# Inverse deviations spread over the partitions straight from SBUF, in place of a bounce through DRAM

## The chip, the cores and the metric

The kernel runs on one NeuronCore of a Trainium2 chip. The metric is the device time of one execution in microseconds (us). Before the change the median of three runs is 1423.2 us (1422.77 to 1428.34).

## What is computed

The input `x` is 32 images of 64 channels, 56 by 56 pixels, float32. A binarised 3x3 convolution with batch normalisation is added first; then each pixel, seen as a token of 64 channels, is normalised over its channels and goes through eight small expert networks. Cut to what matters here:

```python
x = x + conv_block(_ln_c(x), ...)                  # sign(x) * sign(w), batch norm, clip to [-1, 1]
t = _to_tokens(x)                                  # [32, 3136, 64]
u = (t - mean(t, -1)) / sqrt(var(t, -1) + 1e-5)    # _ln_t: over the 64 channels of one token
feat = mean(u, axis=0)                             # over the 32 images
w = softmax(feat @ Wr + br, axis=-1)               # one gate of 8 per pixel position
h = relu(bn1(u @ W1 + b1)); h = relu(bn2(h @ W2 + b2)); y = h @ Wo + bo    # 8 experts
x = _from_tokens(t + sum_over_experts(y * w))
```

The change lies in how `1/sqrt(var + 1e-5)`, one number per token, reaches the 64 partitions that hold the channels of that token.

## The kernel before, in words

SBUF has 128 partitions. Channels lie on partitions twice: partitions 0 to 63 hold the 64 channels of the even image rows, 64 to 127 those of the odd ones (`h` = 0 and 1). The first stage, up to about 204 us of the profile, is the convolution over 32 images; it leaves its output `y` in SBUF. The second stage is a sequence of 28 chunks (`body_of_chunks`, `RP` = 28), each with two image rows of all 32 images. All loops of this stage are unrolled. Each engine has a program of its own, and they meet in semaphores.

Within a chunk, 8 units (`u`) with 6 points each (48 half-points `h`) run the three expert layers: TensorE does `layer1`, `layer2` and `layer3` (L550, L572, L588), ScalarE evicts layer 1 (L743), VectorE evicts layer 2 and applies the gates (L936). Between these, `prep_point` puts the preparation of the next two chunks at half-points written out by hand in the table `STEADY`, which is counted over two chunks: an entry of 48 or more lies in the chunk just ahead of the one that is prepared, at that number less 48. For chunk `q` = `k` + 1, prepared during chunk `k`:

- `var` = 52: four matmuls (L614) sum the squares over the channels; ScalarE makes logarithm, copy, exponential and square of the result (L770 to L777), the inverse deviations `rs`;
- `inv` = 60 and 62: VectorE corrects them by one Newton step (L963 to L968) and signals `rs_done`. `rs` then holds eight useful rows of 448 floats (1792 bytes): partition 32*i + h is the row for image group i (0 to 3) and half h;
- `spread_rs` (L296 to L305), on SyncE (SP) whose queue issues the DMAs, copies each of these rows to 64 partitions of the tile `spread`. Groups 0 and 1 are step `p` = 0, groups 2 and 3 are `p` = 1;
- `norm` (L432 to L435) on GpSimd (POOL) multiplies the centred tokens `xc` of step `p` by `spread` as soon as `rb_loaded[p]` says that it is there, and signals `u_done[p]`;
- `feature` (L439 to L449), next on POOL, sums the normalised tokens over the images (four additions), which needs both steps, and signals `feat_done`;
- `logits` = 87: TensorE waits for `feat_done` and multiplies by the gate weights (L626); softmax, `turn` (L633) and `wb` (L639) follow at 90 to 95, before the next chunk's first units need the gates.

The order on POOL in a chunk is written out too: three `add_const`, the last group's `add_upper` of the chunk before, `add_const`, `add_upper(k, 0)`, then the two `norm` and `feature` of chunk k + 1, then `add_upper(k, 1)` and `add_upper(k, 2)` (L465), after each of which SP stores a quarter of the chunk. SP's order is: load of the first half of chunk k + 2 (L287), store of the chunk before (L312), load of the second half, `spread_rs` of chunk k + 1, three stores. The tile `spread` has a second use: ScalarE writes the squares of chunk k + 2 into it (L762, at half-points 33 and 45 of chunk k) after waiting for `u_done[p]` of chunk k + 1.

The normalisation of chunk 0 has no chunk to hide in: it runs between the end of the convolution and the first unit (`prep_ahead`), and so do `spread_rs(0, 0)` and its two `norm`.

Of the kernel before, what the change touches and what calls it, by code (L numbers as in the profile page):

```python
# [5 lines left out]
F32 = mybir.dt.float32  # L6
# [9 lines left out]
B, C, H, W = 32, 64, 56, 56  # L16
# [8 lines left out]
STEPS = 2  # L25
G = 4
BG = B // G
NG = BG * W
# [22 lines left out]
def metaformer_kernel(nc, x, cw, gamma, beta, Wr, br, W1, b1, g1, be1, m1, v1, W2, b2, g2, be2, m2, v2, Wo, bo, out):  # L51
    with ExitStack() as ctx:
        def sb(name, shape, dt, to=ctx):
            return to.enter_context(nc.sbuf_tensor(name, shape, dt))

        def sem(name):
            return ctx.enter_context(nc.semaphore(name))
# [37 lines left out]
        h = sb("h", [P, 2, 2, 2, NG], F32)  # L95
# [16 lines left out]
        o = sb("o", [P, B, W], F32)  # L112
        t = sb("t", [P, G, NG], F32)
        xc = sb("xc", [P, 2, STEPS, 2, NG], F32)
        spread = sb("spread", [P, STEPS, 2, NG], F32)
        rs = sb("rs", [P, NG], F32)
# [9 lines left out]
        wb = sb("wb", [P, 2, PAIRS, 2, W], F32)  # L126
        gconst = sb("gconst", [P, 2, W], F32)

        rs_rows = nc.dram_tensor("rs_rows", [2, 2, STEPS, 2, NG], F32).ap()

        ps = ctx.enter_context(nc.psum_tensor("ps", [P, 8, 512], F32))
        L1_BANKS, L2_BANKS, ACC_BANKS = 0, (2, 4), 6
# [34 lines left out]
        root_done = sem("root_done")  # L167
        rs_done = sem("rs_done")
        d_rs = sem("d_rs")
        rs_kept = sem("rs_kept")  # L170
        rb_loaded = [sem(f"rb_loaded{p}") for p in range(STEPS)]
        u_done = [sem(f"u_done{p}") for p in range(STEPS)]
        feat_done = sem("feat_done")
# [54 lines left out]
        def body_of_chunks(chunk):  # L228

            for k in range(RP):  # L230
                chunk(k, k % 2, k == 0, min(RP - 1 - k, 2))
# [26 lines left out]
        with nc.Block() as block:  # L258


            @block.sync
            def _(sp):
                for s in stored:
                    sp.sem_inc(s, 16)
                for h in range(2):
                    sp.dma_start(cwt[64 * h:64 * h + 64], cw).then_inc(s_cw, 16)
                    sp.dma_start(gb[64 * h:64 * h + 64, 0:1], gamma.rearrange("(c o) -> c o", o=1)).then_inc(s_cw, 16)

                def load_image(b, slot):

                    xb = x_pairs[b] if isinstance(b, int) else x_pairs[bass.ds(b, 1)].rearrange("o c k t w -> (o c) k t w")
                    sp.dma_start(xa[0:64, slot, 1:SLOTS, :], xb[:, :, 1, :]).then_inc(s_xa[slot], 16)
                    sp.dma_start(xa[64:128, slot, 0:RP, :], xb[:, :, 0, :]).then_inc(s_xa[slot], 16)

                sp.wait_ge(s_zero, 1)
                for b in range(XRING):
                    load_image(b, b)
                with sp.Fori(0, B // XRING - 1) as r:
                    for i in range(XRING):
                        sp.wait_ge(a_split, XRING * r + i + 1)  # L280
                        load_image(XRING * r + XRING + i, i)

                def load_half(q, s, p):
                    images = slice(2 * BG * p, 2 * BG * p + 2 * BG)
                    xq = x[images, :, bass.ds(2 * q, 2), :] if not isinstance(q, int) else x[images, :, 2 * q:2 * q + 2, :]
                    for h in range(2):
                        sp.dma_start(xin[64 * h:64 * h + 64, s, images], xq[:, :, h, :].rearrange("b c w -> c b w")).then_inc(x_loaded[p], 16)  # L287

                sp.wait_ge(a_split, B - XRING + XIN_OVER)
                for q in range(2):  # L290
                    for p in range(STEPS):
                        if q:
                            sp.wait_ge(x_loaded[p], 32)
                        load_half(q, q, p)

                def spread_rs(q, s):  # L296

                    sp.wait_ge(rs_done, q + 1)
                    for i in range(2 * STEPS):
                        sp.dma_start(rs_rows[s, :, i // 2, i % 2], rs[32 * i:32 * i + 2, :]).then_inc(rs_kept, 16)  # L300
                    sp.wait_ge(rs_kept, 32 * STEPS * q + 32 * STEPS)
                    for p in range(STEPS):
                        for h in range(2):
                            sp.dma_start(spread[64 * h:64 * h + 64, p],
                                         rs_rows[s, h, p:p + 1].broadcast_to([C, 2, NG])).then_inc(rb_loaded[p], 16)  # L305

                def store(k, g):
                    images = slice(BG * g, BG * g + BG)
                    oq = out[images, :, bass.ds(2 * k, 2), :] if not isinstance(k, int) else out[images, :, 2 * k:2 * k + 2, :]
                    sp.wait_ge(sum_done, G * k + g + 1)  # L310
                    for h in range(2):
                        sp.dma_start(oq[:, :, h, :].rearrange("b c w -> c b w"),  # L312
                                     o[64 * h:64 * h + 64, images]).then_inc(stored[g], 16)

                def chunk(k, s, first, left):
                    if left > 1:
                        sp.wait_ge(x1g_done, G * k + 2)
                        load_half(k + 2, s, 0)
                    if not first:
                        store(k - 1, G - 1)  # L320
                    if left > 1:
                        sp.wait_ge(x1g_done, G * k + G)
                        load_half(k + 2, s, 1)
                    if left:
                        spread_rs(k + 1, 1 - s)
                    for g in range(G - 1):
                        store(k, g)
                    if not left:
                        store(k, G - 1)

                spread_rs(0, 0)
                body_of_chunks(chunk)
                for s in stored:
                    sp.wait_ge(s, 32 * RP + 16)
# [3 lines left out]
            def _(pool):  # L338
# [92 lines left out]

                def norm(q, s, p):  # L432

                    pool.wait_ge(rb_loaded[p], 32 * q + 32)
                    nc.gpsimd.tensor_tensor(xc[:, s, p], xc[:, s, p], spread[:, p], ALU.mult).then_inc(u_done[p], 1)  # L435

                FEAT_STEPS = 3
# [29 lines left out]
                def chunk(k, s, first, left):  # L467
                    for g in range(G - 1):
                        add_const(k, s, g)
                    if not first:  # L470
                        add_upper(k - 1, G - 1)
                    add_const(k, s, G - 1)
                    add_upper(k, 0)
                    if left:
                        for p in range(STEPS):
                            norm(k + 1, 1 - s, p)
                        feature(k + 1, 1 - s)
                    add_upper(k, 1)
                    add_upper(k, 2)
                    if not left:  # L480
                        add_upper(k, G - 1)

                for p in range(STEPS):
                    norm(0, 0, p)
# [552 lines left out]
```

## Time and profile before

| | |
|---|---|
| median of 3 runs | 1423.2 us |
| the profiled execution's own time | 1421.64 us |
| its span, first to last instruction | 1419.7 us |
| TensorE busy | 1344.9 us (95%) |
| VectorE, ScalarE, GpSimd busy | 971.1, 885.3, 553.2 us |
| moved by DMA | 107.08 MB, mean 75 GB/s |
| mean granted TensorE clock | 0.984 |

All times below are of the one profiled execution, counted from the start of its span. A row of a timeline gives the start, the duration, the engine, the source line, the operation, the output tile and its inputs, and in brackets the idle time of the engine before it with what ended that. Issue instructions on SP show when a DMA is handed over, not when its data lands.

### The profile page before, as it was taken

Reading aid. Unit: us, or ns where it says so; the run is one execution under the profiler, and the core shown is the slowest. Engines: PE = TensorE matmul, PEld = TensorE weight load, DVE = VectorE, ACT = ScalarE, POOL = GpSimd, SP = SyncE. Lnnn points to the kernel's source line nnn. Section 1 sums busy time; section 2 is a strip of 40 time slices with the busy share of each in tenths; the row PEclk is TensorE's granted clock in tenths of the full one; section 3 lists DMA queues with packets and bytes.
Section 4 is the critical chain, followed back from the end, with each engine's and each line's share of the span. In section 5 each row is a group of like instructions: output and inputs, shape, how many; then the busy total and the mean of one; then the engine's idle time right before and its main releaser. Section 6 shows DMA issues by size and latency. Waiting matters only on the chain. (4 is left out here: it accounts for less than half of the span.)

```text
span 1419.7 us, 34136 instructions
## 1 busy us (share of the span) xinstructions
PE 1344.9 (95%) x12984; PEld 667.3 (47%) x12984; DVE 971.1 (68%) x1660; ACT 885.3 (62%) x1279; POOL 553.2 (39%) x474
## 2 busy tenths in 40 slices
PE   3999973999999999999999999999999999999998
PEld 2666651544444544445444444444544454444444
DVE  5888872676767666666666666676766767666665
ACT  3666664666666666656666666666666666666653
POOL 7000052434444443444343344444434444434441
PEclk9999995999999999999999999999999999999999
DMA  9999931232233333223333233233333323332221
GB/s 159 176 151 149 143 52 27 60 79 61 55 71 67 73 73 80 52 61 73 67 72 75 61 65 68 62 78 69 77 66 61 66 60 73 73 80 48 53 49 32
DMA packets 361597, 107.08 MB, mean 75 GB/s; under 512 B 353552, under 2 KB 353776, under 8 KB 361456
## 3 DMA queue, kind: packets, MB, share of 16 engines
q1 hardware_dynamic: 360192, 103.49, 38.9%
q0 software_dynamic: 1264, 1.61, 0.7%
q8 instruction: 101, 1.65, 0.5%
q14 instruction: 40, 0.33, 0.1%
HBM read 78.97 MB, written 26.09 MB: 74 GB/s over the span
## 5 line engine op out<-in xcount | busy, mean ns | idle before, releaser
L936 DVE SCALAR_TENSOR_TENSOR v<-ps,negb,wb 128x448 f32<-128x448 f32 x896 | 571.0, 678 | 300.9 <-PE ps L572 300.1
L743 ACT ACTIVATE h<-ps,bias 128x896 f32<-128x896 f32 x448 | 451.3, 1007 | 318.9 <-PE ps L550 318.9
L550 PE MATMUL ps<-xc,w 64*64 64x448 f32 x3584 | 458.1, 541 | 13.1 <-POOL xc L435 11.3
L588 PE MATMUL ps<-v,wo 64*64 64x448 f32 x3584 | 454.7, 540 | 3.4 <-issue 2.9
L572 PE MATMUL ps<-h,w 64*64 64x448 f32 x3584 | 450.9, 540 | 4.9 <-issue 2.5
L588 PEld LDWEIGHTS ps<-v,wo 64*64 64x64 f32 x3584 | 169.9, 133 | 187.5 <-issue 174.6
L550 PEld LDWEIGHTS ps<-xc,w 64*64 64x64 f32 x3584 | 162.3, 132 | 185.2 <-issue 179.4
L572 PEld LDWEIGHTS ps<-h,w 64*64 64x64 f32 x3584 | 166.0, 133 | 160.3 <-issue 146.7
L465 POOL TENSOR_TENSOR o<-o,upper 128x448 f32<-128x448 f32 x112 | 127.4, 1137 | 284.3 <-DVE o L946 284.3
L457 POOL TENSOR_TENSOR o<-xin,gconst 128x448 f32<-128x448 f32 x112 | 130.2, 1182 | 236.0 <-ACT gconst L786 143.3
L435 POOL TENSOR_TENSOR xc<-xc,spread 128x896 f32<-128x896 f32 x56 | 121.5, 2187 | 172.0 <-DMA spread<-rs_rows 172.0
L518 PE MATMUL ps<-sgn,convw 128*128 128x392 bf16 x768 | 135.1, 332 | 0.0
L712 ACT ACTIVATE y<-ps 128x392 f32 (+1 forms) x128 | 63.3, 498 | 59.8 <-PE ps L518 59.8
L518 PEld LDWEIGHTS ps<-sgn,convw 128*128 128x128 bf16 x768 | 72.6, 98 | 55.7 <-issue 6.2
L749 ACT ACTIVATE upper<-ps 128x448 f32<-128x448 f32 x112 | 60.5, 541 | 55.5 <-PE ps L588 55.5
L957 DVE SCALAR_TENSOR_TENSOR xin<-t,xin 128x448 f32<-128x448 f32 x112 | 88.5, 793 | 1.0 <-ACT t L767 0.9
L875 DVE BATCH_NORM_STATS2 stats<-y (+1 forms) x128 | 69.0, 562 | 22.5 <-ACT y L712 22.1
L767 ACT ACTIVATE t<-y,bn 128x448 f32<-128x448 f16 x112 | 83.3, 749 | 0.1
L946 DVE TENSOR_TENSOR o<-ps,o 128x448 f32<-128x448 f32 x112 | 68.9, 615 | 18.6 <-PE ps L588 18.6
L606 PE MATMUL ps<-xin,centre 64*64 64x448 f32 x448 | 62.5, 560 | 7.2 <-DVE xin L957 4.3
L758 ACT ACTIVATE xc<-ps 128x896 f32<-128x896 f32 x56 | 51.4, 918 | 28.4 <-PE ps L606 28.4
L704 ACT ACTIVATE sgn<-ps 128x392 bf16<-128x392 f32 (+1 forms) x128 | 55.5, 526 | 13.9 <-PE ps L509 13.7
(151 smaller groups left out, 837.8 us busy)
## 6 DMA issues: line engine op xcount, KB each, us to landing
xa<-in_x SPq DMA_DIRECT2D x64, 392.0 KB, 6.3
xin<-in_x SPq DMA_DIRECT2D x112, 224.0 KB, 4.1
spread<-rs_rows SPq DMA_DIRECT2D x112, 224.0 KB, 4.1
out<-o SPq DMA_DIRECT2D x224, 112.0 KB, 2.5
rs_rows<-rs SPq DMA_DIRECT2D x112, 3.5 KB
rows<-in_L_ffn_g POOLq DMA_DIRECT2D x2, 256.0 KB, 6.1
rows<-in_L_ffn_v POOLq DMA_DIRECT2D x2, 256.0 KB, 7.2
cwt<-in_L_conv_weight SPq DMA_DIRECT2D x2, 144.0 KB, 2.6
```

What stands on the lines that cost most here:

```text
L435: nc.gpsimd.tensor_tensor(xc[:, s, p], xc[:, s, p], spread[:, p], ALU.mult).then_inc(u_done[p], 1)
L457: nc.gpsimd.tensor_tensor(o[:, images, :], xin[:, s, images, :], gconst[:, s:s + 1, :].broadcast_to([P, BG, W]), ALU.add).then_inc(x1g_don ...
L465: nc.gpsimd.tensor_tensor(og, og, upper[:], ALU.add).then_inc(sum_done, 1)
L518: last = mm(at, convw[:, kx, nxt, :], sgn[:, i % 2, KG * g + nxt:KG * g + nxt + KG, kx:kx + W], start=(kx + nxt == 0), stop=(kx + nxt == 3))
L550: last = mm(ps[64 * two:64 * two + 64, L1_BANKS + ab, 0:NG], w1[half, P * q + C * two:P * q + C * two + C], xc[half, s, g // 2, ab ^ (g % ...
L572: last = mm(ps[64 * i:64 * i + 64, L2_BANKS[ab] + low, 0:NG], w2[rows_, Q + QUADS * i, :], h[rows_, u % 2, i, ab, :], start=True, stop=True)
L588: last = mm(ps[64 * par:64 * par + 64, ACC_BANKS + low, 0:NG], wo[rows_, 2 * Q + d, :], v[rows_, u % 2, par ^ (g % 2), d, :], start=(Q == ...
L743: A(h[:, u % 2, i], ps[:, L1_BANKS:L1_BANKS + 2, 0:NG], ACT.Relu, bias=bias[:, 0, q:q + 1]).then_inc(h_done[i], 1)
L767: A(t[:, g].rearrange("p (b w) -> p b w", w=W), yq, ACT.Relu, bias=OFFSET1, scale=SCALE).then_inc(t_done, 1)
L875: last = V.bn_stats(sb_, yb)
L936: last = V.scalar_tensor_tensor(out=v[:, u % 2, ab, d, :].rearrange("p (b w) -> p b w", w=W), in0=ps[:, L2_BANKS[ab] + d, 0:NG].rearrange( ...
L957: V.scalar_tensor_tensor(out=xg, in0=t[:, g].rearrange("p (b w) -> p b w", w=W), scalar=2.0, in1=xg, op0=ALU.min, op1=ALU.add).then_inc(x1 ...
```

## The change

The DRAM tensor `rs_rows`, its semaphore and the four small DMAs that wrote it are gone, and with them SP's wait for them. Each of the four 224 KB loads, which read two rows of DRAM for 64 partitions, becomes two DMAs of 112 KB; each of these reads one row of `rs`, 1792 bytes on one SBUF partition, 64 times over, and writes it to 64 partitions of `spread`. `rb_loaded[p]` now counts four DMAs.

```diff
-        rs_rows = nc.dram_tensor("rs_rows", [2, 2, STEPS, 2, NG], F32).ap()
...
                     sp.wait_ge(rs_done, q + 1)
                     for i in range(2 * STEPS):
-                        sp.dma_start(rs_rows[s, :, i // 2, i % 2], rs[32 * i:32 * i + 2, :]).then_inc(rs_kept, 16)
-                    sp.wait_ge(rs_kept, 32 * STEPS * q + 32 * STEPS)
-                    for p in range(STEPS):
                         for h in range(2):
-                            sp.dma_start(spread[64 * h:64 * h + 64, p],
-                                         rs_rows[s, h, p:p + 1].broadcast_to([C, 2, NG])).then_inc(rb_loaded[p], 16)
+                            sp.dma_start(spread[64 * h:64 * h + 64, i // 2, i % 2],
+                                         rs[32 * i + h:32 * i + h + 1, :].rearrange("o (a n) -> o a n", a=1).broadcast_to([1, C, NG])).then_inc(rb_loaded[i // 2], 16)
...
-                    pool.wait_ge(rb_loaded[p], 32 * q + 32)
+                    pool.wait_ge(rb_loaded[p], 64 * q + 64)
```

The order on SP, in the program before, around the first two calls of `spread_rs` (the tile `xin` takes the input for the residual):

```order
L287 DMA xin<-in_x 64x16x56
L300 DMA rs_rows<-rs 2x448 [waits rs_done]
L300 DMA rs_rows<-rs 2x448 x3
L304 DMA spread<-rs_rows 64x896 [waits rs_kept]
L304 DMA spread<-rs_rows 64x896 x3
L287 DMA xin<-in_x 64x16x56 [waits x1g_done]
```

The same place in the changed program, up to the stores of the first chunk (its lines are numbered two to five lower):

```order
L285 DMA xin<-in_x 64x16x56
L299 DMA spread<-rs 64x1x448 [waits rs_done]
L299 DMA spread<-rs 64x1x448 x7
L285 DMA xin<-in_x 64x16x56 [waits x1g_done]
L285 DMA xin<-in_x 64x16x56
L285 DMA xin<-in_x 64x16x56 [waits x1g_done]
L285 DMA xin<-in_x 64x16x56
L299 DMA spread<-rs 64x1x448 [waits rs_done]
L299 DMA spread<-rs 64x1x448 x7
L307 DMA out<-o 64x8x56 [waits sum_done]
```

Eight DMAs with one wait stand where there were eight with two; what comes before and after them on SP is the same, and no other engine's order moves.

## Rows read from the trace of the kernel before

**Rows 1.** The page: the span, and the engines' busy time in it

```profile
span 1419.7 us, 34136 instructions
PE 1344.9 (95%) x12984; PEld 667.3 (47%) x12984; DVE 971.1 (68%) x1660; ACT 885.3 (62%) x1279; POOL 553.2 (39%) x474
```

**Rows 2.** Windows by stage: us, busy of each engine, PEclk, DMA share, GB/s

```profile
840.91:881.57 40.66, 40.53 (x430) 17.92 (x433) 27.98 (x52) 27.09 (x36) 17.91 (x14) 1.00 0.33 70
256.29:1340.23 1083.94, 1070.04 (x11072) 503.29 (x11074) 742.01 (x1326) 703.21 (x936) 467.28 (x362) 1.00 0.32 68
```

**Rows 3.** Waits of all engines: us in total, times, longest us

```profile
POOL xc L435 <- DMA spread<-rs_rows: 172.0, 30, 25.7
...
PE ps L550 <- POOL xc L435: 11.3, 1, 11.3
...
PE ps L626 <- POOL feat L449: 4.6, 5, 2.0
```

**Rows 4.** Waits of SP's queue: us in total, times, longest us

```profile
SPq L304 <- DMA rs_rows<-rs: 64.4, 28, 2.7
```

**Rows 5.** Timeline of a middle chunk: SP, POOL, ScalarE and TensorE

```profile
766.20 1.13 SPq L300 DMA_DIRECT2D rs_rows<-rs  x4
769.68 2.40 SPq L304 DMA_DIRECT2D spread<-rs_rows  x4
...
774.46 4.46 POOL L435 TENSOR_TENSOR xc<-xc,spread 128x896 f32<-128x896 f32 x2 [5.18 <-DMA spread<-rs_rows]
779.05 2.08 POOL L444 TENSOR_TENSOR feat<-xc 128x896 f32<-128x896 f32 x1
...
783.44 0.42 POOL L449 TENSOR_TENSOR feat<-feat 128x112 f32<-128x112 f32 x1
783.82 1.14 POOL L465 TENSOR_TENSOR o<-o,upper 128x448 f32<-128x448 f32 x1
...
782.06 0.94 ACT L762 ACTIVATE spread<-xc 128x896 f32<-128x896 f32 x1
...
785.51 0.34 PE L626 MATMUL ps<-wr,feat 64*56 64x8 f32 x7
```

**Rows 6.** Timeline of two other chunks: end of the feature, start of the logits

```profile
867.42 0.42 POOL L449 TENSOR_TENSOR feat<-feat 128x112 f32<-128x112 f32 x1
868.07 0.34 PE L626 MATMUL ps<-wr,feat 64*56 64x8 f32 x7
...
1199.65 0.42 POOL L449 TENSOR_TENSOR feat<-feat 128x112 f32<-128x112 f32 x1
1202.16 0.34 PE L626 MATMUL ps<-wr,feat 64*56 64x8 f32 x7
```

**Rows 7.** Timeline ahead of the first chunk

```profile
227.48 1.19 SPq L300 DMA_DIRECT2D rs_rows<-rs  x4
...
229.62 2.40 SPq L304 DMA_DIRECT2D spread<-rs_rows  x4
...
234.41 4.10 POOL L435 TENSOR_TENSOR xc<-xc,spread 128x896 f32<-128x896 f32 x2 [25.66 <-DMA spread<-rs_rows]
236.62 1.77 PE L550 MATMUL ps<-xc,w 64*64 64x448 f32 x8 [11.34 <-POOL xc L435]
...
242.74 0.42 POOL L449 TENSOR_TENSOR feat<-feat 128x112 f32<-128x112 f32 x1
...
244.49 0.38 PE L626 MATMUL ps<-wr,feat 64*56 64x8 f32 x8
...
260.56 0.96 PE L588 MATMUL ps<-v,wo 64*64 64x448 f32 x8
```

**Rows 8.** DMA issues: KB each, median us from issue to landing

```profile
spread<-rs_rows SPq DMA_DIRECT2D x112, 224.0 KB, 4.1
out<-o SPq DMA_DIRECT2D x224, 112.0 KB, 2.5
rs_rows<-rs SPq DMA_DIRECT2D x112, 3.5 KB
```

**Rows 9.** Windows in bursts of the spread: DMA share and GB/s last

```profile
230.50:233.50 3.00, 0.00 (x0) 0.00 (x0) 0.00 (x0) 0.00 (x0) 0.00 (x0) 0.50 0.86 209
270.40:270.90 0.50, 0.50 (x10) 0.45 (x8) 0.50 (x2) 0.41 (x1) 0.00 (x0) 1.00 0.52 208
```

**Rows 10.** Windows ahead of the first chunk: TensorE idle, then busy again

```profile
226.00:228.00 2.00, 0.00 (x0) 0.00 (x0) 1.93 (x5) 2.00 (x4) 0.00 (x0) 1.00 0.00 0
230.00:232.00 2.00, 0.00 (x0) 0.00 (x0) 0.00 (x0) 0.00 (x0) 0.00 (x0) 0.50 0.51 129
250.00:252.00 2.00, 2.00 (x14) 0.72 (x15) 0.00 (x0) 0.65 (x2) 0.50 (x1) 0.50 0.00 0
252.00:254.00 2.00, 1.71 (x16) 0.66 (x12) 0.55 (x1) 1.01 (x1) 2.00 (x3) 0.86 0.00 0
```

More of the change, by code:

```diff
@@ L169, in metaformer_kernel @@
         d_rs = sem("d_rs")
-        rs_kept = sem("rs_kept")
         rb_loaded = [sem(f"rb_loaded{p}") for p in range(STEPS)]
```

## The prediction
> **What bounds the kernel now.** I read the page first: TensorE is busy for 1344.9 of 1419.7 us [rows 1]. The windows by stage say how closely: over 26 chunks it works 1070.04 of 1083.94 us at the full clock, so a chunk lasts 41.7 us, and in the best one it works 40.53 of 40.66 us [rows 2]. In these chunks nothing but TensorE's own work can be shortened by more than half a microsecond each. The list of waits then shows who could hold it up. POOL waits 172.0 us for the spread rows, the longest wait on a DMA [rows 3], but POOL is not the bound, so that costs nothing by itself. What it leads to costs: TensorE waits 4.6 us in 5 places for the sum over the images, and 11.3 us once, ahead of the first chunk, for the first normalised tokens [rows 3].
>
> The timeline of a middle chunk gives the path and its slack. SP hands over the small DMAs at 766.20, waits for them, hands over the four loads from 769.68; POOL starts `norm` at 774.46, ends the feature at 783.86, and TensorE takes it at 785.51 [rows 5]. From SP's first issue to the end of the feature that is 17.7 us. The slack behind it is 1.65 us here; over the 28 chunks it runs from 0.2 (868.07 less 867.84) to 2.1 us (1202.16 less 1200.07) [rows 6], and I take 0.9 us for all. So this path is off the critical one by less than a microsecond: saving on it buys almost nothing, and a delay beyond 0.9 us is paid in full, once per chunk.
>
> **What goes.** The four small DMAs and the wait for them: 3.48 us from 766.20 to 769.68 [rows 5], with 64.4 us of waiting over the 28 calls [rows 4]. Nothing that TensorE does depends on them except through this path.
>
> **What comes.** Eight DMAs of 112 KB where four of 224 KB stood. Four loads are handed over in 2.40 us [rows 5], 0.6 each, so eight take 4.8 us; that ends at 4.8 us after the first issue, where before it ended at 5.9. The issue is no price. The stores queued behind them on SP can be handed over a microsecond earlier.
>
> The price is the transfer. The bytes that are written stay the same: 8 x 64 x 1792 = 917,504. What is new is where they are read: each of the eight DMAs reads one row on a single SBUF partition, 64 times, for all DMA engines at once. No row of this trace shows many engines on one partition. The bounds, from the nearest rows: at best it goes as from DRAM, where a load lands 4.1 us after its issue [rows 8] and the burst runs at 209 GB/s [rows 9]. At worst one partition serves its readers one after the other, at what one DMA engine draws: in the best half-microsecond of a burst a busy engine moves 208 / (0.52 x 16) = 25 GB/s, over three microseconds 209 / (0.86 x 16) = 15 GB/s [rows 9]. The small DMAs, two partitions each, are the only reads of `rs` in the trace, 3.5 KB each [rows 8], too short to say which holds; the stores [rows 8] draw on 64 partitions at once.
>
> I take the one-engine rate, the better value of 25 GB/s, because the sixteen engines reach 209 GB/s in the loads of before with all of DRAM behind them and 64 partitions in front, while here the whole burst has one narrow source at a time. 917,504 bytes at 25 GB/s are 36.7 us. A rule of the Trainium skill speaks against the change in the same way ("SBUF — State Buffer", section "Door 1: The DMA port swizzle"): partitions share 16 DMA ports of about 27.2 GB/s each, and by its formula rows 0, 1, 32 and 33 lie on one port and 64, 65, 96 and 97 on another. By that figure the transfer would be an estimated 33.7 us and the sum below 84 us less; if the two ports worked side by side it would be 17 us. No row here tells these apart.
>
> **The sum.** Data starts to flow about 1 us after the first issue (in 230 to 232 us the engines are busy for half of the window, the first load having been handed over at 229.62) [rows 7, 10]. The last row lands 37.7 us after the first issue; `norm` of the second step takes 2.1 us (half of the 4.10 of both) [rows 7]; from the end of `norm`, 778.92, to the end of the feature, 783.86, it is 4.9 us [rows 5]. Together 44.7 us, against 17.7 plus 0.9 of slack: TensorE waits 26.1 us at the logits of each of 27 chunks, 705 us. Some of this wait moves forward, since ScalarE may not write the next squares into `spread` (782.06) [rows 5] before `norm` is done; it is the same wait, not a second one. `add_upper` of the next group stands behind the feature on POOL (783.82) [rows 5]; its 1.1 us and its store come later by the same 26 us, and the stop of TensorE covers them.
>
> Ahead of the first chunk, SP starts at 227.48 and the feature ended at 243.16; now it ends at 272.2, less 1.3 us of slack before 244.49 [rows 7]: 28 us. The first `norm` no longer decides there, since the feature needs both steps.
>
> TensorE's clock: it stops at full clock (1.00 in 226 to 228), is granted half (0.50, 1.2 of 2.4 GHz) while still idle in 230 to 232, and after a stretch of steady work from 250 us is at 0.86 in 252 to 254 [rows 10]. Eight matmuls take 1.77 us at half and 0.96 us at full clock [rows 7]. I charge 1.5 us for each of 28 stops, 42 us; the bounds are 0 and 4 us (0 to 112).
>
> 1421.6 (the profiled execution) + 705 + 28 + 42 = 2197 us; I say **2195 us**. The median of the runs shown, 1423.2, is 1.6 us above the profiled one.
>
> **The rivals.**
>
> *Unhindered.* The direct read goes as fast as the read from DRAM. Then the path shortens by about 2 us: p = 0 lands about 2.5 us after its fourth issue at 2.4 us [rows 5, 8], 5 us in place of the 6.9 between 227.48 and 234.41 [rows 7]. The head gains 2 us, the 5 waits of 4.6 us [rows 3] go, and the time is 1415 us. It speaks for it that the bytes, the engines and the written partitions are the same; against it, the single source. It decides at 0.9 us of slack: the transfer may last 17.7 + 0.9 - 2.1 - 4.9 - 1 = 10.6 us, 87 GB/s, before TensorE feels it; above that rate the change is never slower. The Trainium skill has a rule on that side as well ("DMA: Bandwidth & Descriptors", section "Where 436 GB/s comes from"): between SBUF and SBUF the fabric's 435 GB/s binds, an estimated 2.1 us for these bytes. Chance 0.17.
>
> *In part hindered.* A partition gives more than one engine's worth, or the two pairs of rows flow side by side, two to three and a half times 25 GB/s. At 50 GB/s the transfer is 18.4 us, the feature ends after 26.4 us, 7.8 too late: 28 x 7.8 = 218, 1640 us, up to 1680 with the clock. At 75 GB/s it is 12.2 us, 1.6 too late, 1467 us. Chance 0.05.
>
> *Worse than one engine's best.* Readers disturb each other and the burst runs at 20 GB/s: 45.9 us, 9.2 more for each of 28, 2450 us. It belongs to the forecast's own range.
>
> **How the numbers follow.** One source at a time: 0.78, its own range 1800 to 2450 us, with about 0.02 above it. In part: 0.05, of which the part above 1600 is in the range. Unhindered: 0.17, left out whole. The range is 1600 to 2450 us. About 0.5% (7 us) is what a measurement of this kernel can tell from no change. The unhindered case, 1415 us, is 0.45 to 0.6% below, so it is split: 0.07 faster, 0.10 the same; all else, 0.83, is slower.
>
> **What would show it.** In the profile after: landing of the spread's DMAs far above 4.1 us, growing from the first to the eighth, with a DMA share near 1 and only about 25 GB/s for some 37 us in each chunk; POOL's wait for `spread` near 28 x 30 us; TensorE waiting for the feature (or for ScalarE behind `norm`) some 25 us in every chunk, chunks of about 68 us; the granted clock at half after each stop. The forecast is wrong if the landing stays below some 10 us, in which case TensorE's 41 us per chunk stand and only the head moves; its size is wrong if the burst's GB/s is far from 25.

## The result and the profile after

The changed kernel takes 2085.14 us (median of 4 runs, 2084.86 to 2086.99) against 1423.45 us before: a ratio of 1.4625 (95% interval 1.4593 to 1.4658). It is 662 us slower; 2195 was forecast, 1600 to 2450 the range.

The page of the changed kernel answers to [rows 1]:

```profile
span 2082.9 us, 34136 instructions
PE 1476.5 (71%) x12984; PEld 739.5 (36%) x12984; DVE 962.5 (46%) x1660; ACT 885.8 (43%) x1279; POOL 539.1 (26%) x474
```

The windows by stage, to be read beside the second row of [rows 2] (us, busy time of each engine, granted clock, DMA share, GB/s): the first is the same 26 chunks, from the first to the last ScalarE read of the variances; the second is four microseconds within one burst of the spread, when the input's load had landed and no store had been handed over.

```profile
282.47:1977.94 1695.47, 1193.35 (x11072) 573.33 (x11074) 733.02 (x1326) 703.64 (x935) 454.89 (x362) 0.84 0.54 43
1016.00:1020.00 4.00, 2.12 (x12) 0.98 (x15) 0.44 (x1) 0.00 (x0) 0.00 (x0) 0.69 0.87 27
```

A chunk now lasts 1695.47 / 26 = 65.2 us, 23.5 more than before. The DMA engines are busy for 87% of that window and move 27 GB/s, where they moved 209 GB/s at 86% [rows 9]: they wait for data. The list of waits, to be read beside [rows 3]:

```profile
POOL xc L430 <- DMA spread<-rs: 814.4, 56, 37.2
...
PE ps L621 <- POOL feat L444: 353.9, 27, 16.6
PE ps L583 <- issue: 65.7, 14, 7.9
...
PE ps L545 <- issue: 53.1, 13, 6.8
...
ACT spread L757 <- POOL xc L430: 37.0, 9, 6.6
PE ps L567 <- issue: 34.9, 9, 8.4
...
PE ps L545 <- POOL xc L430: 22.9, 1, 22.9
```

TensorE's wait for the feature has grown from 4.6 to 353.9 us, in 27 places: 13.1 us each. The timeline of a middle chunk of the changed kernel, in the order of [rows 5]:

```profile
1009.54 23.18 SPq L299 DMA_DIRECT2D spread<-rs  x8
1032.77 24.50 SPq L307 DMA_DIRECT2D out<-o  x6
...
1028.00 2.08 POOL L430 TENSOR_TENSOR xc<-xc,spread 128x896 f32<-128x896 f32 x1 [15.38 <-DMA spread<-rs]
1043.54 2.07 POOL L430 TENSOR_TENSOR xc<-xc,spread 128x896 f32<-128x896 f32 x1 [13.45 <-DMA spread<-rs]
...
1049.82 0.42 POOL L444 TENSOR_TENSOR feat<-feat 128x112 f32<-128x112 f32 x1
...
1050.39 0.42 PE L621 MATMUL ps<-wr,feat 64*56 64x8 f32 x5 [9.72 <-POOL feat L444]
```

The two `norm` start 18.5 and 34.0 us after SP's first issue, and the feature ends after 40.7 us, where it took 17.7. In the DMA issues, against [rows 8], the landing has gone from 4.1 to 14.4 us for half the bytes per DMA:

```profile
spread<-rs SPq DMA_DIRECT2D x224, 112.0 KB, 14.4
out<-o SPq DMA_DIRECT2D x224, 112.0 KB, 2.5
```

The stores read 64 partitions per DMA and land as before. So reading SBUF by DMA is not slow as such. What is slow about these reads was open: the number of DMAs (theory C below), the way from SBUF to SBUF (D), the single partition (A2), or the DMA port on which that partition lies (A1).

### The profile page after: what moved, and what is told of

It is laid out like the page before. It is cut to its first block and busy times, and to the rows that moved or that the text cites. A ratio compares the mean times of both kernels' runs of the same rounds, so it can differ in the third digit from the quotient of the medians.

```text
span 2082.9 us, 34136 instructions
## 1 busy us (share of the span) xinstructions
PE 1476.5 (71%) x12984; PEld 739.5 (36%) x12984; DVE 962.5 (46%) x1660; ACT 885.8 (43%) x1279; POOL 539.1 (26%) x474
## 5 line engine op out<-in xcount | busy, mean ns | idle before, releaser
L545 PE MATMUL ps<-xc,w 64*64 64x448 f32 x3584 | 519.7, 580 | 76.0 <-issue 53.1
L583 PE MATMUL ps<-v,wo 64*64 64x448 f32 x3584 | 523.6, 588 | 66.2 <-issue 65.7
L567 PE MATMUL ps<-h,w 64*64 64x448 f32 x3584 | 520.3, 590 | 37.3 <-issue 34.9
L430 POOL TENSOR_TENSOR xc<-xc,spread 128x896 f32<-128x896 f32 x56 | 116.2, 2075 | 814.4 <-DMA spread<-rs 814.4
L583 PEld LDWEIGHTS ps<-v,wo 64*64 64x64 f32 x3584 | 197.9, 144 | 273.5 <-issue 253.9
L545 PEld LDWEIGHTS ps<-xc,w 64*64 64x64 f32 x3584 | 189.6, 144 | 268.2 <-issue 256.9
L621 PE MATMUL ps<-wr,feat 64*56 64x8 f32 x224 | 15.7, 238 | 364.5 <-POOL feat L444 353.9
L567 PEld LDWEIGHTS ps<-h,w 64*64 64x64 f32 x3584 | 187.7, 145 | 207.4 <-issue 191.4
L621 PEld LDWEIGHTS ps<-wr,feat 64*56 64x56 f32 x224 | 13.9, 198 | 389.4 <-issue 389.2
L941 DVE TENSOR_TENSOR o<-ps,o 128x448 f32<-128x448 f32 x112 | 69.4, 620 | 40.1 <-PE ps L583 39.8
L601 PE MATMUL ps<-xin,centre 64*64 64x448 f32 x448 | 72.8, 607 | 19.7 <-issue 14.3
## 6 DMA issues: line engine op xcount, KB each, us to landing
spread<-rs SPq DMA_DIRECT2D x224, 112.0 KB, 14.4
```

Of the source, the lines that this page charges most:

```text
L545: last = mm(ps[64 * two:64 * two + 64, L1_BANKS + ab, 0:NG], w1[half, P * q + C * two:P * q + C * two + C], xc[half, s, g // 2, ab ^ (g % ...
L567: last = mm(ps[64 * i:64 * i + 64, L2_BANKS[ab] + low, 0:NG], w2[rows_, Q + QUADS * i, :], h[rows_, u % 2, i, ab, :], start=True, stop=True)
L583: last = mm(ps[64 * par:64 * par + 64, ACC_BANKS + low, 0:NG], wo[rows_, 2 * Q + d, :], v[rows_, u % 2, par ^ (g % 2), d, :], start=(Q == ...
L601: last = mm(ps[64 * high:64 * high + 64, Z + low, 0:NG], centre64[rows_, :], xin[rows_, s, BG * g:BG * g + BG, :], start=True, stop=True)
L941: V.tensor_tensor(og, ps[:, ACC_BANKS, 0:NG], og, ALU.add).then_inc(out_done, 1)
```

## The experiments

The kernel before was timed beside each experiment on the same chip; ratios are against that.

### The split alone

The kernel before, its loads from DRAM halved (`rb_loaded[p]` counts four DMAs here too):

```diff
                         for h in range(2):
-                            sp.dma_start(spread[64 * h:64 * h + 64, p],
-                                         rs_rows[s, h, p:p + 1].broadcast_to([C, 2, NG])).then_inc(rb_loaded[p], 16)
+                            for a in range(2):
+                                sp.dma_start(spread[64 * h:64 * h + 64, p, a],
+                                             rs_rows[s, h, p, a:a + 1].broadcast_to([C, NG])).then_inc(rb_loaded[p], 16)
...
```

> The kernel before with its four loads from DRAM split into eight of 112 KB, as the change has them; the bounce through DRAM stays. Theory A (the single SBUF source is what costs): the time stays at 1423 us, within 5 us, since the eight hand-overs take some 5 us of SP in place of 2.4 and the path has under 1 us of slack in some chunks; landing near 4 us. Theory C (eight DMAs of 112 KB are what costs, by number or by form): near the changed kernel, above 1700 us.

1427.99 us, ratio 1.0011 (0.9997 to 1.0025). Eight DMAs in this form cost nothing that can be told. TensorE waits for the feature 11.2 us in 12 places in place of 4.6 in 5, which shows how little slack there is. Theory C falls.

### Sixteen source partitions per DMA

Each row of `rs` exists 16 times, since the variance matmul (same shape, 565 ns in place of 566) now fills all its 32 columns:

```diff
-                    nc.gpsimd.memset(var_ones[64 * h:64 * h + 64, h:h + 3:2], 1.0 / C).then_inc(s_const, 1)
+                    nc.gpsimd.memset(var_ones[64 * h:64 * h + 64, h:32:2], 1.0 / C).then_inc(s_const, 1)
...
-                                         rs[32 * i + h:32 * i + h + 1, :].rearrange("o (a n) -> o a n", a=1).broadcast_to([1, C, NG])).then_inc(rb_loaded[i // 2], 16)
+                                         rs[32 * i + h:32 * i + 32:2, :].rearrange("o (a n) -> o a n", a=1).broadcast_to([16, C // 16, NG])).then_inc(rb_loaded[i // 2], 16)
```

> The changed kernel with each row of rs made 16 times over (the weights of the variance matmul filled in all 32 columns, alternating by half, at no cost on TensorE), and each of the eight DMAs reads 16 partitions, two apart, four times each, in place of one partition 64 times. Theory A (one port or one partition is the source that saturates): the burst runs above 150 GB/s, POOL's first norm starts about 5 to 6 us after SP's first issue, and the time is 1412 to 1423 us. Theory D (a copy from SBUF to SBUF is slow in itself): it stays above 1800 us.

1424.79 us, ratio 0.9995 (0.9981 to 1.0008). A window inside a burst, and the DMA issues, of this run:

```profile
600.60:604.60 4.00, 4.00 (x48) 1.84 (x44) 3.06 (x6) 3.14 (x4) 1.79 (x2) 1.00 0.97 221
...
spread<-rs SPq DMA_DIRECT2D x224, 112.0 KB, 2.8
```

221 GB/s in all, of which the spread's own packets are 200 (the rest is the end of the input's load), from SBUF to SBUF, to the same destinations: theory D falls, and the whole 662 us are the narrow source. But the 1412 to 1423 us that a fast read was to give did not come; that question is taken up below.

### Four sources, adjacent or apart

On top of the filled columns, the source alone differs:

```diff
-rs[32 * i + h:32 * i + 32:2, :].rearrange("o (a n) -> o a n", a=1).broadcast_to([16, C // 16, NG])
+rs[32 * i:32 * i + 4, :].rearrange("o (a n) -> o a n", a=1).broadcast_to([4, C // 4, NG])
```

for the adjacent ones (half of the copies then carry the rows of the other half `h`, which changes what is computed but no order or size), and for those apart

```diff
-rs[32 * i + h:32 * i + 32:2, :].rearrange("o (a n) -> o a n", a=1).broadcast_to([16, C // 16, NG])
+rs[32 * i + h:32 * i + 32:8, :].rearrange("o (a n) -> o a n", a=1).broadcast_to([4, C // 4, NG])
```

> As the kernel with 16 sources, but each DMA reads the four adjacent partitions 32*i to 32*i+3, each 16 times; only every second of these rows belongs to the half it is written to, so the normalisation of the tokens gets deviations of the other half in part. Theory A1 (the limit belongs to the DMA port, which adjacent partitions share): burst near 29 GB/s, 2050 to 2110 us. Theory A2 (the limit belongs to the single partition or its address): four times the rate, near 100 GB/s or what four DMA engines draw, 9 us of transfer, 1415 to 1450 us.

> As the kernel with four sources, but the four partitions are eight apart (32*i + h and 8, 16 and 24 above it), which by the map of the SBUF page lie on four ports. Theories A1 and A2 agree: near 100 GB/s, 9 us of transfer, the feature ends 17 us after SP's first issue as before, 1415 to 1450 us. If four sources mean only that four DMA engines take part and these are slow by themselves, it is far above that, and the run with four adjacent sources says nothing on the port.

Adjacent: 2213.87 us, ratio 1.5526 (1.5476 to 1.5575), above the expected 2050 to 2110. Eight partitions apart: 1453.0 us, ratio 1.0190 (1.0157 to 1.0223), just above the expected 1450. The waits of the second, and a window inside one of its bursts:

```profile
POOL xc L430 <- DMA spread<-rs: 228.1, 56, 25.4
...
PE ps L621 <- POOL feat L444: 29.6, 26, 2.4
...
656.00:660.00 4.00, 4.00 (x42) 2.35 (x39) 2.75 (x6) 1.38 (x3) 1.29 (x1) 1.00 0.26 98
```

Both use four partitions, each read 16 times, in the same number of DMAs. Only the distance between the partitions differs, and it makes 761 us. Theory A2, a limit of the single partition, falls: four adjacent ones together are no faster than one. The limit is shared by neighbours, as a port is; that it is the port and not something else with the same grouping, no run can tell. The adjacent run is in fact slower than one partition read 64 times; both `norm` of a chunk show by how much:

```profile
642.03 24.03 SPq L299 DMA_DIRECT2D spread<-rs  x8
...
662.19 2.07 POOL L430 TENSOR_TENSOR xc<-xc,spread 128x896 f32<-128x896 f32 x1 [17.07 <-DMA spread<-rs]
...
679.82 2.07 POOL L430 TENSOR_TENSOR xc<-xc,spread 128x896 f32<-128x896 f32 x1 [15.57 <-DMA spread<-rs]
```

The second starts 37.8 us after the first issue; less about 1 us of start, 917,504 bytes in 36.8 us are 25 GB/s, against 28 in the changed kernel (33.0 us in the chunk above). Windows inside this burst, the first with other traffic in it, the second without, show a DMA share of a quarter, as much as four engines of sixteen, where the changed kernel has 0.87:

```profile
645.00:675.00 30.00, 16.26 (x163) 9.34 (x152) 10.86 (x18) 10.15 (x12) 2.19 (x2) 0.80 0.25 31
650.00:656.00 6.00, 6.00 (x69) 4.47 (x65) 4.25 (x8) 3.71 (x5) 0.00 (x0) 1.00 0.23 25
```

The run with the partitions apart has the same share, 0.26, and moves 98 GB/s with it. So the number of DMA engines at work does not explain the adjacent run. In these traces a packet of the spread (one row, 1792 bytes) takes 74 ns with the partitions apart, 260 ns with four adjacent ones and 928 ns in the changed kernel (medians inside a burst): the more engines draw on one place, the longer each of them waits for the same row.

### Half of it direct

Step 0 by the direct read, step 1 through DRAM:

```diff
-                    for i in range(2 * STEPS):
+                    for i in range(2, 4):
                         sp.dma_start(rs_rows[s, :, i // 2, i % 2], rs[32 * i:32 * i + 2, :]).then_inc(rs_kept, 16)
+                    for i in range(2):
+                        for h in range(2):
+                            sp.dma_start(spread[64 * h:64 * h + 64, 0, i],
+                                         rs[32 * i + h:32 * i + h + 1, :].rearrange("o (a n) -> o a n", a=1).broadcast_to([1, C, NG])).then_inc(rb_loaded[0], 16)
-                    sp.wait_ge(rs_kept, 32 * STEPS * q + 32 * STEPS)
-                    for p in range(STEPS):
+                    sp.wait_ge(rs_kept, 32 * q + 32)
+                    for p in (1,):
...
-                    pool.wait_ge(rb_loaded[p], 32 * q + 32)
+                    pool.wait_ge(rb_loaded[p], (64, 32)[p] * (q + 1))
```

> Step 0 direct from one SBUF partition per DMA as in the changed kernel, step 1 by the bounce through DRAM as before: half of the narrow reads. If the price is bytes over the rate of one port, the narrow part lasts 15.5 us (half of the 31 of the changed kernel), the rest 2 to 3 us behind it in the same rings; the feature ends 1 + 15.5 + 2.5 + 2.1 + 4.9 = 26 us after SP's first issue, 7.4 us too late, 28 times: 1630 us, up to 1670 with the clock. If the price were a fixed one per chunk, not one per byte, it would be near 2085 us.

1727.97 us, ratio 1.2146 (1.2034 to 1.2258): above the 1630 to 1670 that were expected. A chunk of it:

```profile
645.89 0.81 SPq L300 DMA_DIRECT2D rs_rows<-rs  x2
646.75 7.18 SPq L303 DMA_DIRECT2D spread<-rs  x4
653.98 8.38 SPq L308 DMA_DIRECT2D spread<-rs_rows  x2
...
665.42 4.54 POOL L439 TENSOR_TENSOR xc<-xc,spread 128x896 f32<-128x896 f32 x2 [16.44 <-DMA spread<-rs]
...
674.20 0.42 POOL L453 TENSOR_TENSOR feat<-feat 128x112 f32<-128x112 f32 x1
```

The feature ends 28.7 us after SP's first issue, not 26: the small DMAs go first, `norm` of step 0 starts after 19.5 us. That is 10.1 us beyond the 18.6 that are free, 283 us in 28 places; 1424 and 283 make 1707, and the other 21 us fit a clock charge of under a microsecond per stop. Half of the narrow bytes cost 303 of 662 us, so the price goes with the bytes and not with the chunk. The two loads from DRAM took SP 4.2 us each to hand over where the kernel before needs 0.6.

### Eight ports, one per DMA

One partition per DMA again, with the filled columns, but at 0, 5, 40, 45, 80, 85, 120 and 125, so that by the port map named below each of the eight lies on a port of its own ("four apart" in the expectation is the step of the added offset, not the distance):

```diff
-rs[32 * i + h:32 * i + h + 1, :]
+rs[32 * i + h + 4 * (2 * i + h):32 * i + h + 4 * (2 * i + h) + 1, :]
```

> As the changed kernel, one partition per DMA read 64 times, but the eight source partitions are four apart, each on a port of its own by the map of the SBUF page. If the DMA engines work through the DMAs one after the other (rings in order), the one port in use at a time still sets the rate: burst of 28 to 31 us, 1990 to 2085 us. If the DMAs flow side by side, the burst is shorter than 10 us and the time 1420 to 1480 us.

### The order of the groups

```diff
-                    for i in range(2 * STEPS):
+                    for i in (0, 2, 1, 3):
```

> The changed kernel with its eight DMAs in the order groups 0, 2, 1, 3: DMAs of the one port (groups 0 and 1) alternate with those of the other (2 and 3), two by two. If rings in order set the pace: both steps end near 30 us, so the feature ends as in the changed kernel, 2060 to 2100 us, a little more since the first norm starts later and ScalarE waits for it longer. If the two ports work side by side: burst near 16 us, 1600 to 1680 us.

The first took 1645.77 us (ratio 1.1568, 1.1412 to 1.1724), the second 1909.35 us (1.3421, 1.3311 to 1.3530). Neither is where one of the two theories put it. A chunk of the kernel with a port per DMA:

```profile
620.17 12.48 SPq L299 DMA_DIRECT2D spread<-rs  x8
631.86 2.08 POOL L430 TENSOR_TENSOR xc<-xc,spread 128x896 f32<-128x896 f32 x1 [8.61 <-DMA spread<-rs]
638.04 2.28 POOL L430 TENSOR_TENSOR xc<-xc,spread 128x896 f32<-128x896 f32 x1 [4.10 <-DMA spread<-rs]
```

and of the interleaved one:

```profile
636.86 19.60 SPq L299 DMA_DIRECT2D spread<-rs  x8
...
657.56 2.09 POOL L430 TENSOR_TENSOR xc<-xc,spread 128x896 f32<-128x896 f32 x1 [17.61 <-DMA spread<-rs]
...
663.94 2.07 POOL L430 TENSOR_TENSOR xc<-xc,spread 128x896 f32<-128x896 f32 x1 [4.29 <-DMA spread<-rs]
```

Less 1 us of start, the transfers last 16.9 and 26.1 us, where the changed kernel's last 33.0. By the port map of the Trainium skill ("SBUF — State Buffer", section "Door 1: The DMA port swizzle") the source moves to another port once in the changed kernel, 3 times in the interleaved one and 7 times here. Per further passage that is (33.0 - 26.1) / 2 = 3.5 and (26.1 - 16.9) / 4 = 2.3 us saved (3.1 and 2.3 by the means of 27 chunks, 32.4, 26.2 and 17.0). So a DMA and the one behind it in the queue do overlap, as long as they draw on different ports, but far from all eight at once. This says again that it is the port: the changed kernel's groups 0 and 1 read partitions 0, 1, 32 and 33, four different ones, and gain nothing from the overlap: on average the first three DMAs of the changed kernel land 4.2 us apart, 27 GB/s, and only towards the one passage the steps get shorter (3.4 and 3.7 us). If 32 and 33 were elsewhere than 0 and 1, the changed kernel would have had the interleaved one's three passages, and its time.

### Why the fast direct read gains nothing, and a version that does

With 16 sources the path is shorter than in the kernel before, and the time is the same. The groups of that kernel that changed:

```profile
L952 DVE SCALAR_TENSOR_TENSOR xin<-t,xin 128x448 f32<-128x448 f32 x112 | 125.4, 1123 | 1.0 <-ACT t L762 0.9
L601 PE MATMUL ps<-xin,centre 64*64 64x448 f32 x448 | 62.4, 576 | 11.7 <-issue 6.0 <-DVE xin L952 4.3 <-ACT xc L753 1.1
```

VectorE's addition on the residual (`x1`) takes 1123 ns; in the kernel before the same groups read:

```profile
L957 DVE SCALAR_TENSOR_TENSOR xin<-t,xin 128x448 f32<-128x448 f32 x112 | 88.5, 793 | 1.0 <-ACT t L767 0.9
L606 PE MATMUL ps<-xin,centre 64*64 64x448 f32 x448 | 62.5, 560 | 7.2 <-DVE xin L957 4.3 <-issue 1.6 <-ACT xc L758 1.1
```

Now that POOL starts `norm` earlier, its work falls onto more of the `x1`; in the changed kernel, where POOL mostly waits, they take 678 ns. The Trainium skill has a rule for such a meeting ("SBUF — State Buffer", section "Who interferes with whom"): a two-input operation of VectorE and one of GpSimd that reads SBUF exclude each other on a shared pair of ports. The durations agree: an `x1` that meets no instruction of POOL takes at most 626 ns in every kernel here (70 of them in the kernel before, 34 with 16 sources), and one that meets POOL up to 2.5 us (42 of mean 1090 ns, and 78 of mean 1343). That the two exclude each other, and do not merely slow each other down, no run measured.

What this does to TensorE shows in one distance. After the third `x1` of a chunk VectorE has two evictions `v` to do, and with 16 sources TensorE's first centring matmul (L601) starts 1.29 us after the end of that `x1` in 23 of 27 chunks; in the kernel before it does so in 3. The profile puts this idle time down to "issue", ten times and 4.3 us in all, in place of once. From the logits of the second chunk to those of the last, the windows of the kernel before and of the one with 16 sources read:

```profile
283.48:1366.80 1083.32, 1069.81 (x11072) 500.33 (x11069) 740.50 (x1322) 699.51 (x930) 469.62 (x365) 1.00 0.32 67
282.39:1368.51 1086.12, 1074.39 (x11075) 496.80 (x11069) 770.75 (x1322) 699.89 (x930) 475.98 (x364) 1.00 0.33 67
```

Its idle time has fallen from 13.5 to 11.7 us (the waits for the feature went from 4.6 to 0.3 us, the ones behind `x1` came), but it is busy for 4.6 us more with the same matmuls at the same clock. The held matmuls may be part of that, but no row says so.

I went on from a wider form of the direct read, one DMA of 224 KB per group:

```diff
-                    nc.gpsimd.memset(var_ones[64 * h:64 * h + 64, h:h + 3:2], 1.0 / C).then_inc(s_const, 1)
+                    nc.gpsimd.memset(var_ones[64 * h:64 * h + 64, 16 * h:16 * h + 16], 1.0 / C).then_inc(s_const, 1)
...
-                        for h in range(2):
-                            sp.dma_start(spread[64 * h:64 * h + 64, i // 2, i % 2],
-                                         rs[32 * i + h:32 * i + h + 1, :].rearrange("o (a n) -> o a n", a=1).broadcast_to([1, C, NG])).then_inc(rb_loaded[i // 2], 16)
+                        sp.dma_start(spread[:, i // 2, i % 2],
+                                     rs[32 * i:32 * i + 32, :].rearrange("o (a n) -> o a n", a=1).broadcast_to([32, 4, NG])).then_inc(rb_loaded[i // 2], 16)
...
-                    pool.wait_ge(rb_loaded[p], 64 * q + 64)
+                    pool.wait_ge(rb_loaded[p], 32 * q + 32)
```

> The weights of the variance matmul filled so that 16 of each 32 rows of rs belong to the one half and 16 to the other; one DMA per group reads 32 partitions four times each and writes all 128 partitions of spread: four DMAs of 224 KB, no bounce. Hand-over 2.4 us in place of 4.8. Transfer as fast as in the kernel with 16 sources; if what held that one back is that its norm meets VectorE's additions on the residual (its L952 took 1123 ns against 793 in the kernel before), this one is no better: 1421 to 1427 us. If the hand-over mattered: 1415 to 1420 us.

1425.61 us, ratio 1.0005 (0.9994 to 1.0016): no gain. Then three tries with the table, on top of it, the first being

```diff
-            t=(12, 15, 18, 21), x1=(20, 24, 26, 32), centre=(31, 43), power=(33, 45),
+            t=(4, 7, 18, 21), x1=(9, 12, 30, 34), centre=(31, 43), power=(33, 45),
```

> The kernel with four wide DMAs, and VectorE's additions on the residual (x1) moved out of the stretch in which POOL now runs norm and feature: half-points 9, 12, 30, 34 in place of 20, 24, 26, 32, and ScalarE's t at 4, 7, 18, 21. If the collision of VectorE and POOL took the gain away, x1 takes under 750 ns, TensorE no longer waits for it at L601, and the time is 1408 to 1418 us, better than the kernel before. If TensorE's own work sets a chunk, it stays at 1420 to 1427 us. If ScalarE or VectorE is now late at the units where t and x1 were put, it is slower than 1430 us.

1432.54 us, ratio 1.0063 (1.0048 to 1.0079). The meeting did become rarer (910 ns in place of 1071), yet the time rose. The second, `x1=(20, 24, 30, 34)` and `t` as it was:

> The kernel with four wide DMAs, with only the second pair of VectorE's residual additions moved: half-points 20, 24, 30, 34 in place of 20, 24, 26, 32, so that the third no longer falls into POOL's feature. If the meeting with POOL costs, x1's mean falls from 1071 ns and the time is 1 to 5 us below the kernel with four wide DMAs. If TensorE's own work and its eviction set a chunk, no change, 1421 to 1428 us.

1419.3 us beside 1427.41 us of the kernel before: ratio 0.9948 (0.9929 to 0.9966), the one kernel of the study that is faster. The third, `t=(8, 11, 18, 21)`, `x1=(13, 16, 30, 34)`:

> As before, with both pairs outside POOL's norm and feature (x1 at 13, 16, 30, 34) and t at 8, 11, 18, 21, closer to the old places than in the slower try with 9 and 4. If it was the early places (4 to 9, beside the load of the input and POOL's additions) that cost 7 us there, this one is at 1415 to 1423 us; if any place away from the tuned ones costs, near 1432 us.

1438.62 us, ratio 1.0083 (1.0064 to 1.0102). What each does to TensorE is in the groups of `x1` and of the centring matmuls behind it. With four wide DMAs and the old table:

```profile
L951 DVE SCALAR_TENSOR_TENSOR xin<-t,xin 128x448 f32<-128x448 f32 x112 | 119.6, 1071 | 1.0 <-ACT t L761 0.9
L600 PE MATMUL ps<-xin,centre 64*64 64x448 f32 x448 | 62.3, 573 | 10.3 <-issue 4.9 <-DVE xin L951 4.3 <-ACT xc L752 1.1
```

with the late pair:

```profile
L951 DVE SCALAR_TENSOR_TENSOR xin<-t,xin 128x448 f32<-128x448 f32 x112 | 117.7, 1054 | 1.0 <-ACT t L761 0.9
L600 PE MATMUL ps<-xin,centre 64*64 64x448 f32 x448 | 62.9, 568 | 6.8 <-DVE xin L951 4.3 <-issue 1.4 <-ACT xc L752 1.1
```

and with both pairs moved (the `x1` group, and a row of the list of waits):

```profile
L951 DVE SCALAR_TENSOR_TENSOR xin<-t,xin 128x448 f32<-128x448 f32 x112 | 84.6, 758 | 1.0 <-ACT t L761 0.9
...
PE ps L582 <- DVE v L930: 21.4, 26, 1.2
```

The last of these is the clearest: `x1` is quicker than in the kernel before (758 ns against 793), but its first pair, put at half-points 13 and 16, stands beside the Newton step (half-points 12 and 14) and delays VectorE's eviction `v` ahead of layer 3, and TensorE waits for that in 26 places. So the length of `x1` was the wrong measure; where it stands in VectorE's queue counts. In the kernel with the late pair it is no shorter (1054 ns against 1071) and its third one still meets POOL, but it is no longer ahead of the first centring matmul: that starts 1.29 us behind it in 12 of 27 chunks with the old table, in none with the new one. The idle time before L600 falls from 10.3 to 6.8 us, back to about the 7.2 of the kernel before. What puts the late pair ahead of the kernel before is then the shorter path itself. The same stretch as above reads

```profile
282.74:1361.45 1078.71, 1069.38 (x11074) 510.44 (x11069) 763.18 (x1322) 699.95 (x930) 479.12 (x364) 1.00 0.32 67
```

TensorE is busy as long as in the kernel before and idle for 9.3 us in place of 13.5: the waits for the feature are gone. That and 0.7 us ahead of it are the 5.0 us between the two profiled executions (spans of 1414.7 and 1419.7 us). The last run is the control:

> The kernel before, DRAM bounce and all, with the second pair of residual additions moved as in the faster kernel (20, 24, 30, 34). If the table alone gave the 0.5%, this one is at 1416 to 1421 us as well, and the wide direct read adds nothing. If the gain needs the earlier norm, it stays at 1422 to 1430 us: the norm and feature of the kernel before run later, so the third addition at half-point 30 meets them.

1424.62 us, ratio 1.0001 (0.9986 to 1.0016). The table alone gives nothing on top of the DRAM bounce. The 0.5% need both, the shorter way for the inverse deviations and the later pair.

## Why the prediction was right, step by step

**The bound and the slack** held. The path from `rs` to the logits decides as soon as it exceeds 17.7 + 0.9 us. The kernel with four sources apart is the finest test. Its second `norm` starts 12.6 us after SP's first issue (mean of 27 chunks), 11.6 less the start, 79 GB/s, where 10.6 us and 87 GB/s were said to be the limit: a microsecond too late, 28 us, and it costs 26.

**One source at a time, at one engine's rate**, was the right mechanism with the wrong owner and a size off. It was taken for the limit of a partition; the pair of runs with four sources showed that neighbours share it, and the two with other ports that partitions further off do not. The term was 36.7 us at 25 GB/s; it measured 33.0 in the middle chunk (second `norm` at 34.0 us after the issue) and 32.4 on average, 28 GB/s. That the number for one engine came so near is luck: all sixteen engines were at work on the row (share 0.87), and what they shared gave 27 GB/s, while one engine alone, with the partitions apart, drew 98 / (0.26 x 16) = 24 GB/s. Two different limits lie close together here. The estimate by the port figure of the Trainium skill, 33.7 us and 84 us off the sum, which is 2113, was nearer than mine; the measured 2085 lies 28 us below it, on the side of the one passage between ports that overlaps. The trace agrees with the figure: away from the passage, DMAs landed 4.2 us apart, 27 GB/s.

**The sum.** From SP's first issue to the end of the feature 44.7 us were forecast; 40.7 were measured in the chunk shown and 40.1 on average of the 27 behind the first (17.7 before). TensorE takes the feature 0.15 us later, so the path costs 21.7 us per chunk in place of 26.1. The rest of a chunk, from the logits to SP's next issue, grew from 23.1 to 25.0 us with TensorE idle for 0.2 us of it both times: 1.9 us per chunk for the clock, where 1.5 were charged. Together that is the growth of the windows, 611.5 us in 26 chunks (1695.47 - 1083.94), 23.5 each. Ahead of the first chunk 26 us were added in place of 28. In all, 27 x 21.7 = 586 and 50 and 26 are 662 of the 663.2 us by which the span grew; 775 were forecast. The path, too long by 4.4 us in 27 chunks, 119 us, is more than the whole miss of 110 us: the clock, charged too low, took some of it back.

**The clock.** TensorE's busy time grew by 131.6 us for the same 12984 matmuls, three times my 42 us. The stretches tell where the difference lies:

```profile
1048.00:1050.00 2.00, 0.00 (x0) 0.00 (x0) 0.00 (x0) 0.00 (x0) 1.84 (x3) 0.50 0.00 0
1052.00:1054.00 2.00, 2.00 (x16) 1.22 (x12) 1.28 (x2) 0.00 (x0) 0.00 (x0) 0.50 0.57 112
1054.00:1056.00 2.00, 2.00 (x21) 1.09 (x18) 0.86 (x3) 1.15 (x2) 1.13 (x1) 0.74 0.02 3
```

After the stop TensorE works at half clock (1.2 GHz) from 1050.39 until about 1055, which is paid. But 1016 to 1020, in the middle of the burst and ahead of the stop, stood at 0.69 too, TensorE being busy for 2.12 of the 4 us: what is slow there only shortens the wait that follows. Of the 131.6 us about 50 are paid, the 1.9 us per chunk of the sum above.

**The hand-over** was wrong and cost nothing by itself: 4.8 us were forecast for SP, and it took 23.18. On average SP handed over the fifth to the eighth DMA 7.2, 11.4, 15.6 and 19.1 us after the first, each half a microsecond after the landing of the first to the fourth (6.7, 10.9, 15.1 and 18.5). The store whose data POOL had ready at 1012.63 went out only at 1032.77, within the burst, and nobody waited for it: POOL's wait for the stores is 94.4 us, 92.8 before. Since the later DMAs are handed over late, their landings do not grow up to the eighth, as the prediction had it, but take at most 15.9 us each.

**The sign that failed.** TensorE was to wait for the feature some 25 us in every chunk; it waits 13.1 (353.9 us in 27 places). The path costs 21.7, but TensorE meets part of it earlier, at half clock or idle for "issue" within the burst. All its idle time but 0.2 us per chunk lies between SP's first issue and the logits, so the sum is not touched.

**ScalarE** waited for `norm` before its next squares, 37.0 us in 9 places, and this was part of the same stop. **The head**: SP started 3.2 us later (230.64; nothing ahead of it had changed) and the feature ended 40.2 us on, in place of 44.7.

**The rivals.** Neither came, but the study built both. The unhindered read exists, with 16 or 32 sources, at 200 GB/s, and it gives 1425 us and not the 1415 that were worked out. Its waits for the feature did go, but `x1` got into TensorE's way and TensorE was busy for longer, costs that the sum for this rival did not have. With the late pair, which takes `x1` out of the way, it gives 1419.3 us, 8 below the kernel before beside it. The in-part case is the kernel with a port per DMA: 54 GB/s, 1646 us, where 50 GB/s were priced at 1640 to 1680.

## What to carry to other kernels

Before a DMA broadcasts from SBUF, count the ports behind its source and not the bytes: one row read 64 times ran at 28 GB/s, four adjacent ones at 25, about an eighth of what the same bytes reach from DRAM (209) or from 16 partitions (200), and four rows eight apart at 98. Where a matmul makes the row, let it make copies on many partitions, since its spare columns cost nothing here, and read those. And a path that was tuned against its neighbours, once shortened, has to be placed again: the direct read alone gave nothing, the table alone nothing, both together 0.5%.

## What was not expected of the hardware

- DMAs in one queue overlap with the one behind if their ports differ, and not where they are the same, as far as these three runs show: 33, 26 and 17 us for the same bytes with 1, 3 and 7 changes of port.
- A queue that drains slowly holds SP: eight DMAs took 23.18 us to hand over, in place of 0.6 each (the fifth went out half a microsecond after the first had landed), and even a load from DRAM behind such reads took 4.2.
- Four adjacent partitions, read by four DMA engines, were slower (25 GB/s) than one partition read by all sixteen (28 GB/s). By the map the sources lay on one port each time; why fewer engines get less out of it was not tried.
- In the changed kernel TensorE stands idle for "issue", waiting for nothing that the profile shows, 65.7, 53.1 and 34.9 us ahead of the three layers, in pieces of up to 8.4 us; before, such idle time was under 3 us for each. It lies between SP's first issue and the logits and adds nothing to the time (see the sum). The page of the profile lists a DMA queue by the name `instruction`, with 101 packets of 16 KB in the whole run, and 29 of the 32 such pieces above 1.5 us end 1.2 to 1.6 us after the end of one of these packets; in the kernel with a port per DMA all 14 do. The packets take under 1 us as a rule, so it would be their start that is late, behind the reads. In the run with four adjacent sources, none of the 27 pieces ends so: there another cause, not looked for, is at work.
